# Graph network on one core: an edge stage planned in pairs of chunks, three far and two near per turn, instead of groups of four

## The chip, the cores and the metric

One core of a Trainium2 chip runs the whole program as one launch. The metric is the device time in microseconds; the figures given are the median of three runs, with the lowest and the highest.

## The reference

A graph of 6250 nodes with 128 features and 200000 edges (`src`, `dst`, sorted by `dst`) passes four graph layers, each followed by a residual sum and a layer norm. The change touches the last one, an attention over edges, and the step that plans its work:

```python
row, col = edge_index          # row = src, col = dst
h = relu(x[row] @ W1[:d] + x[col] @ W1[d:] + b1)
mask = sigmoid(h @ W2 + b2)[:, 0]
seg_sum = segment_sum(mask, row, num_segments=n)
w = mask / (seg_sum[row] + 1e-09)
agg = segment_sum(w[:, None] * x[col], row, num_segments=n)
out_emb = where((deg > 0)[:, None], 0.5 * x + 0.5 * agg, x)
return relu(out_emb @ Wl + bl)
```

## The kernel before, in words

The edges are sorted on the chip by the tile of 128 nodes that holds their `src` (`load_columns`, `rank_columns`, `permute_columns`, `bucket_ranges`). A **chunk** is 128 edges of one such tile. Each of the 49 tiles gets an even number of chunks, enough for its edges. Counted from the reference's inputs this gives 1614 chunks. A chunk is **near** when the `dst` nodes of its edges lie in two neighbouring tiles (828 chunks of the 1614), otherwise **far**.

`edge_attention` works in **turns**. For every chunk it needs `u` at the source node, plus, at the target node, `v` and the features `x`. The source part is a matmul of a one-hot matrix with the tile of `u` that stays in SBUF. The target part of a far chunk is gathered row by row from a table in DRAM by an indirect DMA of GpSimd (L1694, 128 rows of 1 KB). That of a near chunk comes from two more matmuls with two neighbouring tiles of `vx` (L1862, L1864). So a far chunk costs one gather, and a near chunk costs two extra matmuls of 256 columns. The operands are fp32, and one such matmul is two records in the profile ("x8" is four chunks).

In the kernel before, one turn is three **groups of four** chunks: two far groups (g = 0, 1) and a near one (g = 2), 12 chunks in all. In step t of the loop (`step` of each engine, buffers `h` alternate):

- PE, for each group: `lookups` of turn t (L1868, or L1862 to L1864 for the near group, into `psz` and `psv`), then `sums` of turn t-1 (L1879, into `psa`), which add the weighted rows up by source node.
- DVE: the one-hots of turn t+1 (L1774). Then, for each group, `z` = matmul + gathered rows (L1807), the adds of turn t-1 from `psa` to the accumulator (L1792, one per pair of chunks), the score with relu and weights (L1819, one per chunk), and the transposed one-hots of turn t+1 (L1778, L1781 for the near ones). For the near group the scores wait for a copy by ACT (`near_x`, L1906).
- ACT: for each group the sigmoid (L1908), then the weighted one-hots (L1914, one per chunk). Before those of the near group it makes `near_x`.
- SP: waits for plan row t+1, loads its numbers into registers, and fetches the broadcast rows for the transposed one-hots (L1708 for `low_rows`, L1709 for `near_rows`). Each time a group's gather of turn t has landed, it fetches the row numbers for that buffer's next gather (L1717). Last it fetches plan row t+2 (L1701).
- POOL: the gathers. It waits for the row numbers and, since the buffers alternate, for the sums of turn t-2.

Which chunks a turn works on stands in a **plan** in DRAM, one row of numbers per turn: tiles for PE, tiles of the sums for DVE, and first columns for SP and DVE. `plan_edges` makes it. Three consecutive groups out of `filled` need one near group (`room` = a third of the groups), and a group counts as near only if all its four chunks are near. With the reference's inputs there are 404 groups, of which 142 are near and 134 are taken as near. The 270 far ones are two per turn and the turns come in twos, so there are 68 trips or 136 turns, with 1088 gathers.

`plan_edges` first finds each group's slot on one partition with DVE operations over 415 elements (L810 to L827). PE turns slots and values into columns (L863, L866, L867). DVE makes one-hots of the slots (L843, L844), PE multiplies them with the values (L872, L875), and five DMAs write the plan (L790 to L794). Nothing else runs beside this step.

At the start of `edge_attention` DVE clears the accumulator (L1752), sets constants (L1754, L1755), copies the low bits of the source (L1756), makes the table row numbers (L1758 to L1760) and stages the first ones (L1767). Only then can the first gather start.

Of the kernel before, what the change touches and what calls it, by code (L numbers as in the profile page):

```python
# [4 lines left out]
F32 = mybir.dt.float32  # L5
# [8 lines left out]
P = 128  # L14
# [18 lines left out]
GROUPS = SC // 4  # L33
assert GROUPS * 21845 < 1 << 24
TURNS = 104
PLAN_ROWS = 212
STEP_W = 36
# [471 lines left out]
def bucket_ranges(nc, m, a):  # L509
# [4 lines left out]
    with ExitStack() as ctx:  # L514
# [10 lines left out]
        keys = sb("keys", [P, 5, NJ], F32)  # L525
# [226 lines left out]
def plan_edges(nc, m):  # L752

    BLK = [(b, min(P, GROUPS - b)) for b in range(0, GROUPS, P)]
    NB4 = len(BLK)
    with ExitStack() as ctx:
        sb = lambda n, s, d=F32: ctx.enter_context(nc.sbuf_tensor("pl_" + n, s, d))
        sem = lambda n: nc.alloc_semaphore("pl_" + n)  # L760
        line = sb("line", [1, 3, SCP])
        ordinal = sb("ordinal", [1, GROUPS])
        narrow, upto, near, taken = (sb(n, [1, GROUPS]) for n in ("narrow", "upto", "near", "taken"))
        to_near, to_far = sb("near_slot", [1, GROUPS]), sb("far_slot", [1, GROUPS])
        half, trips = sb("half", [1, 1]), sb("trips", [1, 1], I32)
        filled, filled_i = sb("filled", [1, 1]), sb("filled_int", [1, 1], I32)
        room, room_i = sb("room", [1, 1]), sb("room_int", [1, 1], I32)
        column = sb("column", [P, NB4])
        axis = sb("axis", [P, 4 * TURNS])
        slots = sb("slots", [P, NB4, 2])  # L770
        of_far, of_near = sb("of_far", [P, NB4, 5]), sb("of_near", [P, NB4, 9])
        far_hot, near_hot = sb("far_hot", [P, NB4, 4 * TURNS]), sb("near_hot", [P, NB4, 2 * TURNS])
        plan = sb("plan", [TURNS, 2, 19], I32)
        none = sb("none", [P, 2 * STEP_W], I32)
        psv = ctx.enter_context(nc.psum_tensor("pl_values_ps", [P, NB4, 16], F32))
        psf = ctx.enter_context(nc.psum_tensor("pl_far_ps", [P, 512], F32))
        psn = ctx.enter_context(nc.psum_tensor("pl_near_ps", [P, 512], F32))
        s_line, s_const, s_none, s_v, s_slots, s_values, s_hots, s_rows, s_plan, s_put = (
            sem(n) for n in ("line", "const", "none", "v", "slots", "values", "hots", "rows", "plan", "put"))
# [74 lines left out]

        @block.tensor
        def _(pe):
            pe.wait_ge(s_line, 16)
            one = m.ones[0:1, 0:1]
            for i, (b, n) in enumerate(BLK):
                for a in (0, 1):  # L860
# [750 lines left out]


def edge_attention(nc, m):

# [474 lines left out]
```

## Time and profile before

| | us |
|---|---|
| median of 3 runs | 4251.69 |
| lowest, highest | 4246.45, 4258.07 |
| the profiled execution's own time | 4245.02 |
| its span in the profile | 4243.3 |
| PE busy, share of the span | 3502.5, 83% |
| DVE busy | 3012.9, 71% |
| ACT busy | 2154.5, 51% |
| POOL busy | 1538.0, 36% |
| mean granted TensorE clock | 0.89 of 2.4 GHz |

The profiled execution is 1.7 us longer than its span and 6.7 us below the median. The shares are averages over stages with different limits, so the edge stage (from 2708 us to about 4150 us) and the plan step (775 to 813 us) are read on their own. "L1868" is a line of the kernel before; "PEld" is the weight load; "issue" is idle time for which the profile shows no releaser. SPq is SP's instruction queue, and its rows are the issuing of DMAs, not their transfer.

### The profile page before, as it was taken

How to read it: one execution, taken by the hardware profiler on the slowest of the kernel's cores; microseconds unless marked ns; L12 is line 12 of the kernel's file. 1: busy time of each engine (PE TensorE's matmuls, PEld its weight loads, DVE VectorE, ACT ScalarE, POOL GpSimd, SP SyncE). 2: the span in 40 equal slices, each digit the busy share in tenths (PEclk: the TensorE clock that was granted, in tenths of full speed). 3: DMA queues.
4: the chain of work that ended last, by engine and by line, in shares of the span. 5: the costliest groups of instructions: out<-in, count | busy, mean ns of one | idle time of the engine just before them, and what ended most of it. 6: DMA issues, size and time to landing. Idle time of an engine off the chain costs nothing. (4 is left out here: it accounts for less than half of the span.)

```text
span 4243.3 us, 93850 instructions
## 1 busy us (share of the span) xinstructions
PE 3502.5 (83%) x20539; PEld 2389.7 (56%) x20540; DVE 3012.9 (71%) x11949; ACT 2154.5 (51%) x6858; POOL 1538.0 (36%) x1256
## 2 busy tenths in 40 slices
PE   4868883698889899995998898688888888888884
PEld 2357782333333344443445344588888888888883
DVE  8999997798888888886002101688888888887785
ACT  0068895256677788885002101455555555555554
POOL 0058884100000000001002001277777777777770
PEclk8855555699999999997999999899999999999996
DMA  2011113001111222221884786355555555555551
GB/s 49 1 10 14 15 17 78 18 26 44 62 70 79 88 96 88 101 92 45 327 304 157 278 303 212 118 151 153 153 151 151 151 151 154 150 150 151 150 148 41
DMA packets 276486, 498.39 MB, mean 117 GB/s; under 512 B 92440, under 2 KB 192943, under 8 KB 276255
## 3 DMA queue, kind: packets, MB, share of 16 engines
q1 hardware_dynamic: 209922, 347.11, 24.4%
q0 software_dynamic: 66336, 149.10, 12.8%
q14 instruction: 191, 1.56, 0.1%
q8 instruction: 37, 0.61, 0.1%
HBM read 391.18 MB, written 104.89 MB: 117 GB/s over the span
## 5 line engine op out<-in xcount | busy, mean ns | idle before, releaser
L1694 POOL DMA_INDIRECT xs<-edge_table,ea_row_stage x1088 | 1085.1, 997 | 345.6 <-issue 329.3
L1245 PE MATMUL a_agg_ps<-a_adj_ring,parts 128*128 128x512 f16 (+1 forms) x2548 | 523.5, 369 | 47.1 <-DMA a_adj_ring<-adjacency 47.0
L1914 ACT ACTIVATE slot_dst<-ea_onehot,ea_mask 128x128 f32<-128x128 f16 x1632 | 535.8, 399 | 13.2
L1044 PE MATMUL ab_agg_ps<-ab_adj_stage,parts 128*128 128x512 f16 x1911 | 529.9, 388 | 0.0
L1868 PE MATMUL ea_psz<-parts,ea_onehot_t 128*128 x2176 | 307.7, 286 | 200.6 <-issue 182.5
L449 ACT ACTIVATE dst_step<-iota,dst_low_bias 128x128 f16<-128x128 f16 x1188 | 358.6, 405 | 216.0 <-PEq L474 213.0
L429 POOL DMA_INDIRECT records<-both_parts,record_row x98 | 350.4, 3576 | 309.9 <-ACT both_parts L455 285.6
L1908 ACT ACTIVATE ea_mask<-ea_dot,b 128x4 f32<-128x4 f32 x408 | 121.3, 297 | 671.0 <-DVE slot_src L1819 666.3
L1385 POOL TENSOR_TENSOR parts<-xs,parts 128x896 f16<-128x896 f32 x7 | 13.2, 1882 | 1226.7 <-ACT parts L1379 1226.7
L1879 PE MATMUL ea_psa<-xs,slot_dst 128*128 128x129 f32 x3264 | 437.5, 278 | 2.5 <-ACT slot_dst L1914 2.5
L1117 ACT ACTIVATE ab_src_off<-iota,ab_neg_src 128x128 f16<-128x128 f16 x712 | 282.2, 396 | 304.1 <-PE ab_adj_ps L1065 141.1
L1245 PEld LDWEIGHTS a_agg_ps<-a_adj_ring,parts 128*128 128x128 f16 x2548 | 242.1, 98 | 328.6 <-DMA a_adj_ring<-adjacency 48.0
L1879 PEld LDWEIGHTS ea_psa<-xs,slot_dst 128*128 128x128 f32 x3264 | 413.8, 194 | 9.8 <-DVE agg_t L1792 2.1
L1868 PEld LDWEIGHTS ea_psz<-parts,ea_onehot_t 128*128 128x128 f32 x2176 | 271.5, 196 | 225.6 <-issue 225.6
L1012 DVE TENSOR_SCALAR ab_dst_hot_middle<-iota,slot_dst 128x512 f16<-128x512 f16 x1218 | 395.0, 349 | 0.0
L1151 ACT ACTIVATE ab_adj_stage<-ab_adj_ps 128x512 f16<-128x512 f32 x637 | 371.9, 605 | 16.4 <-PE ab_adj_ps L1070 14.7
L1065 PE MATMUL ab_adj_ps<-ab_dst_hot_middle,ab_src_hot_middle 128*128 128x512 f16 x1218 | 337.8, 383 | 16.3 <-DVE ab_dst_hot_middle L1012 6.5
L1864 PE MATMUL ea_psv<-vx,xs 128*128 x1088 | 325.0, 380 | 0.0
L1862 PE MATMUL ea_psv<-vx,xs 128*128 x1088 | 324.3, 380 | 0.6 <-DVE xs L1781 0.6
L1044 PEld LDWEIGHTS ab_agg_ps<-ab_adj_stage,parts 128*128 128x128 bf16 x1911 | 190.3, 100 | 228.4 <-issue 19.1
L1792 DVE TENSOR_TENSOR agg_t<-agg_t,ea_psa 128x129 f32 x816 | 230.8, 283 | 96.7 <-PE ea_psa L1879 93.3
L1056 PE MATMUL ab_adj_ps<-ab_dst_hot_first,ab_src_hot_first 128*128 128x512 f16 x637 | 218.5, 391 | 84.7 <-DVE ab_dst_hot_first L1012 50.3
(387 smaller groups left out, 6433.5 us busy)
## 6 DMA issues: line engine op xcount, KB each, us to landing
a_adj_ring<-adjacency SPq DMA_DIRECT2D x182, 896.0 KB, 4.6
ea_low_rows<-low_rows SPq DMA_DIRECT2D x411, 128.0 KB
adjacency<-ab_adj_stage SPq DMA_DIRECT2D x91, 512.0 KB, 2.6
adjacency<-ab_adj_stage SPq DMA_DIRECT2D x91, 384.0 KB, 2.3
ea_near_rows<-near_rows SPq DMA_DIRECT2D x137, 128.0 KB
xs<-edge_table,ea_row_stage POOLq DMA_INDIRECT x1088
edge_table<-vx SPq DMA_DIRECT2D x12, 512.0 KB, 2.9
ea_row_stage<-row_columns SPq DMA_DIRECT2D x272, 2.0 KB
```

The lines of the kernel that those rows point to most:

```text
L429: nc.gpsimd.indirect_dma_start(m.rec[q % 2], bass.IndirectOffsetOnAxis(ap=rows[:, q:q + 1], axis=0), both[:, q, :], None, compute_op=ALU.a ...
L449: ins = nc.scalar.activation(step[:, h, k, :], m.iota128h[:, :], ACT.Sign, bias=m.lo_bias[:, bass.ds(n * K + k, 1)])
L1012: return nc.vector.tensor_scalar(dst[:, k, :], m.iota512[:, :], float(t * SPAN), m.slot_dst[:, bass.ds(c, 1)], ALU.add, ALU.is_equal)
L1044: ins = nc.tensor.matmul(agg_ps[:, :], lhs(r, t), stage[:, k, :], start=start and r == 0, stop=stop and r == parts - 1)
L1065: nc.tensor.matmul(ps[:, k, :], src_m[:, k, :], dst_m[:, k, :], start=False, stop=False).then_inc(s_used_m[k], 1)
L1151: nc.scalar.activation(stage[:, k, :], ps[:, k, :], ACT.Copy, accum_out=col(m.out_deg, n * TG + k)).then_inc(s_taken[k], 1)
L1245: ins = nc.tensor.matmul(ps[:, h, 0:width], lhs(r, t), ring[:, g % SLOTS, k * DB:k * DB + width], start=t == 0 and r == 0, stop=t == NT - ...
L1694: nc.gpsimd.indirect_dma_start(got[:, h, g, k, 0:ROW], None, m.table, bass.IndirectOffsetOnAxis(ap=row_s[:, h, g, k:k + 1], axis=0)).then_ ...
L1864: ins = nc.tensor.matmul(psv[:, k, :, :].rearrange("p c d -> p (c d)"), hot_d[:, 1, k, :], pair(1), start=False, stop=True)
L1868: ins = nc.tensor.matmul(psz[:, g, k, :], hot_t[:, g, k, :], of(m.u, tile_at(tiles[k])), start=True, stop=True)
L1879: ins = nc.tensor.matmul(psa[:, g, k // 2, 0:AW], hot_m[:, g, k, :], what, start=k % 2 == 0, stop=k % 2 == 1)
L1914: ins = nc.scalar.activation(hot_m[:, g, k, :], hot[:, h, g, :, k], ACT.Copy, scale=mask[:, g, k:k + 1])
```

## The change

The unit of the plan is a pair of chunks. A turn has five pairs: far group 0 with two pairs (4 chunks), far group 1 with one pair (2 chunks), and the near group with two pairs (4 chunks). That is 10 chunks, 6 far and 4 near, where it was 12, 8 far and 4 near. A pair counts as near if both chunks are near. From the reference's inputs there are 807 pairs, 337 of them near. `room` is 807 * 409 >> 10 = 322, which leaves 485 far pairs. Turns are (485 + 5) / 6 = 81 trips, or 162 turns, with 162 * 6 = 972 gathers and 162 * 4 = 648 near chunks (before 544).

The two chunks of a pair lie in one tile, so a plan row holds one tile per pair: PE loads 9 numbers instead of 16, DVE 10 instead of 16, SP 8 instead of 6. The broadcast rows are fetched by pair: five DMAs of `low_rows` and two of `near_rows`, each of 128 x 512 B, where there were three and one of 128 x 1 KB. The row numbers for the gathers take three DMAs instead of two.

The plan is made with one-hots of the slots of all chunks (13 blocks of 128 chunks by 840 far and 1120 near slots) which PE sums as the moving operand. The values (tile, first tile, column) are the two or three columns of weights. Eight DMAs with 280 short rows each write the plan from one to three partitions.

At the start of `edge_attention` the row numbers come first, and the clearing of the accumulator last.

```diff
-GROUPS = SC // 4
-TURNS = 104
-PLAN_ROWS = 212
-STEP_W = 36
+PAIRS = SC // 2
+TURNS = 280
+PLAN_ROWS = 284
+STEP_W = 32
...
 def plan_edges(nc, m):
...
-            sp.dma_start(rows_of(1, 0, 16), plan[:, :, 0:16]).then_inc(s_put, 16)
-            sp.dma_start(rows_of(2, 16, 28), plan[:, :, 0:12]).then_inc(s_put, 16)
...
+            sp.dma_start(to(1, 0, 3), far(1)).then_inc(s_put, 16)
+            sp.dma_start(to(2, 16, 3), far(1)).then_inc(s_put, 16)
+            sp.dma_start(to(0, 21, 3), far(0)).then_inc(s_put, 16)
...
-            ch(nc.vector.tensor_reduce(narrow[:, :], line[:, 2, 0:SC].rearrange("o (g k) -> o g k", k=4), AX.X, ALU.min))
+            ch(nc.vector.tensor_reduce(narrow[:, :], line[:, 0:SC].rearrange("o (g k) -> o g k", k=2), AX.X, ALU.min))
...
+            for j in range(NJ):
+                if j >= 4:
+                    dve.wait_ge(s_summed, j - 3)
+                nc.vector.tensor_scalar(far_hot[:, j % 4, :], axis[:, 0:FS], slots[:, j, 1:2], None, ALU.is_equal)
+                nc.vector.tensor_scalar(near_hot[:, j % 4, :], axis[:, :], slots[:, j, 0:1], None, ALU.is_equal).then_inc(s_hot, 1)
+            dve.wait_ge(s_summed, NJ)
+            nc.vector.tensor_scalar(far_v[:, :].rearrange("r (a s) -> r a s", a=2), psf[0:2, :, 0:FH], none_at[0:2, 0:1], None, ALU.add)
...
+            for j in range(NJ):
+                for a in (0, 1):
+                    ins = nc.tensor.matmul(psv[:, j, a:a + 1], slot[0:1, a, j * P:(j + 1) * P], one, start=True, stop=True)
...
+                for b in (0, 1):
+                    nc.tensor.matmul(psf[0:2, b, 0:FH], of_far[:, j, :], far_hot[:, j % 4, b * FH:(b + 1) * FH], start=j == 0, stop=j == NJ - 1)
+                for c, (c0, c1) in enumerate(CUTS):
+                    ins = nc.tensor.matmul(psn[0:3, c, 0:c1 - c0], of_near[:, j, :], near_hot[:, j % 4, c0:c1], start=j == 0, stop=j == NJ - 1)
...
 def edge_attention(nc, m):
+    FAR, NEARBY, KINDS = (0, 1), 2, (0, 1, 2)
+    SIZE, CHUNK, PAIR = (4, 2, 4), (0, 4, 6), (0, 2, 3)
+    CHUNKS, TWOS, FARS = 10, 5, 6
...
-                for g in KINDS:
-                    sp.dma_start(lo[:, h, g, :], m.low_rows[bass.ds(c, G), :]...broadcast_to([P, G * P])).then_inc(s_low[h], 16)
+                for q in range(TWOS):
+                    sp.dma_start(lo[:, h, q, :], rows_at(m.low_rows, base[q])).then_inc(s_low[h], 16)
+                for b, q in enumerate(twos(NEARBY)):
+                    sp.dma_start(rel[:, h, b, :], rows_at(m.near_rows, base[q])).then_inc(s_low[h], 16)
...
-                    nc.vector.tensor_tensor(hot[:, h, g, :, :], lo16[:, bass.ds(c, G)].unsqueeze(1).broadcast_to([P, P, G]), ramp[:, :, :], ALU.is_equal).then_inc(s_hot[g], 1)
+                    for q in twos(g):
+                        ins = nc.vector.tensor_tensor(hot[:, h, q, :, :], lo16[:, bass.ds(column(base[q]), 2)].unsqueeze(1).broadcast_to([P, P, 2]), ramp[:, :, :], ALU.is_equal)
+                    ins.then_inc(s_hot[g], 1)
...
-            nc.vector.memset(m.acc[:, :, :], 0.0)
-            dve.sem_inc(s_add, 16)
-            nc.vector.memset(near_x[:, :, :], 1.0)
...
+            nc.vector.memset(m.acc[:, :, :], 0.0)
+            dve.sem_inc(s_add, 16)
             turns(dve, step, after=after)
```

**SP, one step inside the loop of `edge_attention`**, from the broadcast rows to the next plan row. Before (`ISA` and `REGISTER_ALU` rows are address arithmetic):

```order
L1708 ISA
L1708 DMA ea_low_rows<-low_rows 128x512
L1708 ISA
L1708 DMA ea_low_rows<-low_rows 128x512
L1708 ISA
L1708 DMA ea_low_rows<-low_rows 128x512
L1709 DMA ea_near_rows<-near_rows 128x512
L1714 ISA
L1717 REGISTER_ALU
L1717 DMA ea_row_stage<-row_columns 128x4
L1717 REGISTER_ALU
L1717 DMA ea_row_stage<-row_columns 128x4
```

Now, from the fourth `low_rows` on (three more pairs of rows like the first two stand ahead):

```order
L1709 ISA
L1709 DMA ea_low_rows<-low_rows 128x256
L1709 ISA
L1709 DMA ea_low_rows<-low_rows 128x256
L1711 DMA ea_near_rows<-near_rows 128x256 x2
L1716 ISA
L1719 REGISTER_ALU
L1719 DMA ea_row_stage<-row_columns 128x2
L1719 REGISTER_ALU
L1719 DMA ea_row_stage<-row_columns 128x2
L1716 ISA
L1719 DMA ea_row_stage<-row_columns 128x2
```

Ten DMAs stand between two plan rows where six stood, all on SP's one queue.

**DVE, the start of `edge_attention`.** Before:

```order
L1752 MEMSET agg_t 128x6321
L1754 MEMSET xs 128x528
L1755 MEMSET xs 128x16x4
L1756 CAST ea_src_low<-slot_src 128x1664
L1758 CAST slot_dst<-slot_dst 128x1664
L1759 TENSOR_SCALAR slot_dst<-slot_dst 128x1664
L1760 TENSOR_SCALAR slot_dst<-slot_dst 128x1664
L1662 TENSOR_LOAD ea_steps
L1767 ISA
L1767 COPY ea_row_stage<-slot_dst 128x4
```

Now:

```order
L1756 CAST slot_dst<-slot_dst 128x1664
L1757 TENSOR_SCALAR slot_dst<-slot_dst 128x1664
L1758 TENSOR_SCALAR slot_dst<-slot_dst 128x1664
L1658 TENSOR_LOAD ea_steps
L1763 ISA
L1763 COPY ea_row_stage<-slot_dst 128x2
...
L1841 MEMSET xs 128x528
L1842 MEMSET xs 128x12x4
L1843 CAST ea_src_low<-slot_src 128x1664
...
L1778 TENSOR_SCALAR xs<-ea_near_rows,row_ids 128x512 x2
L1849 MEMSET agg_t 128x6321
```

The accumulator's clearing, two small memsets and one cast left the way of the first gather's row numbers (`ea_row_stage`). The clearing now stands between the first transposed one-hots and the one-hots of turn 1.

## Rows read from the trace of the kernel before

**Rows 1.** The page, costliest groups (part 5): the gathers of the edge stage.
```profile
L1694 POOL DMA_INDIRECT xs<-edge_table,ea_row_stage x1088 | 1085.1, 997 | 345.6 <-issue 329.3
```

**Rows 2.** One tile, `ea_psz`: count, duration ns min/median/max, first and last start us.
```profile
L1868 PE MATMUL ea_psz<-parts,ea_onehot_t x2176: 274/275/577, 2722.5 to 4142.9; 128*128 x198
```

**Rows 3.** Waits, 2800 to 4100 us: total us, times, longest us.
```profile
POOL xs L1694 <- issue: 301.8, 987, 1.2
...
PE ea_psz L1868 <- issue: 164.2, 121, 2.7
...
DVE ea_onehot_t L1778 <- DMA ea_near_rows<-near_rows: 7.2, 20, 1.3
```

**Rows 4.** Windows: us, busy (xcount) PE, PEld, DVE, ACT, POOL; PEclk, DMA, GB/s.
```profile
790.00:813.00 23.00, 12.24 (x68) 12.03 (x67) 3.87 (x26) 0.00 (x0) 0.00 (x0) 0.50 0.02 1
...
2300.00:2600.00 300.00, 269.47 (x1317) 135.71 (x1318) 39.01 (x172) 38.00 (x79) 17.97 (x10) 0.95 0.73 260
...
2700.00:4100.00 1400.00, 1204.44 (x8419) 1125.08 (x8420) 1123.01 (x5272) 707.98 (x2238) 1056.02 (x1059) 0.99 0.52 151
```

**Rows 5.** Timeline of PE, 2690 to 2760 us: start us, us, what, [idle before].
```profile
2744.36 0.60 PE L1862 MATMUL ea_psv<-vx,xs 128*128 x2
...
2748.70 1.05 PE L1879 MATMUL ea_psa<-xs,slot_dst 128*128 128x129 f32 x8
...
2749.60 1.11 PE L1868 MATMUL ea_psz<-parts,ea_onehot_t 128*128 x8
...
2758.83 1.15 PE L1868 MATMUL ea_psz<-parts,ea_onehot_t 128*128 x8 [0.20 <-issue]
```

**Rows 6.** Timeline of all engines, 2746 to 2772 us, same columns.
```profile
2750.27 0.29 DVE L1819 SCALAR_TENSOR_TENSOR slot_src<-ea_psv,w 128x128 f32<-128x128 f32 x1
...
2751.72 0.88 DVE L1781 TENSOR_SCALAR xs<-ea_near_rows,row_ids 128x512 f32<-128x512 f16 x2
...
2760.21 0.29 DVE L1819 SCALAR_TENSOR_TENSOR slot_src<-ea_psv,w 128x128 f32<-128x128 f32 x1 [0.99 <-ACT xs L1906]
...
2761.81 0.88 DVE L1781 TENSOR_SCALAR xs<-ea_near_rows,row_ids 128x512 f32<-128x512 f16 x2
...
2762.93 0.69 PE L1862 MATMUL ea_psv<-vx,xs 128*128 x2 [0.26 <-DVE xs L1781]
```

**Rows 7.** Timeline of the SP queue, 3304 to 3330 us.
```profile
3306.48 0.33 SPq L1717 DMA_DIRECT2D ea_row_stage<-row_columns  x1
3307.16 0.28 SPq L1701 DMA_DIRECT2D ea_steps<-plan_rows  x1
3309.93 1.39 SPq L1708 DMA_DIRECT2D ea_low_rows<-low_rows  x3
3311.41 0.38 SPq L1709 DMA_DIRECT2D ea_near_rows<-near_rows  x1
3312.13 5.34 SPq L1717 DMA_DIRECT2D ea_row_stage<-row_columns  x2
```

**Rows 8.** Timeline of the plan step and what follows it, 760 to 830 us.
```profile
777.82 12.40 PE L863 MATMUL pl_values_ps<-ones,pl_line 1*128 1x1 f32 x64 [12.97 <-DMA pl_line<-chunk_lines]
...
781.01 0.64 DVE L818 SCALAR_TENSOR_TENSOR pl_narrow<-pl_ordinal,pl_filled,pl_narrow 1x415 f32<-1x415 f32 x1
...
786.50 0.36 DVE L827 TENSOR_SCALAR pl_far_slot<-pl_far_slot 1x415 f32<-1x415 f32 x1
...
806.43 0.99 SPq L790 DMA_DIRECT2D plan_rows<-pl_plan  x1
...
809.89 0.25 SPq L794 DMA_DIRECT2D plan_rows<-pl_plan  x1
...
813.08 1.89 DVE L1014 TENSOR_SCALAR ab_neg_src<-slot_src 128x3328 f32<-128x3328 f32 x1 [6.74 <-PEq L2040]
...
816.90 0.87 DVE L1012 TENSOR_SCALAR ab_dst_hot_first<-iota,slot_dst 128x512 f16<-128x512 f16 x3
```

**Rows 9.** Timeline of the start of the edge stage, 2698 to 2740 us.
```profile
2709.22 5.33 DVE L1752 MEMSET agg_t<- 128x6321 f32 x1 [4.43 <-issue]
```

More of the change, by code:

```diff
@@ L760, in plan_edges @@
         sem = lambda n: nc.alloc_semaphore("pl_" + n)
[L761 to L776, printed above, removed]
@@ L777, in plan_edges @@
-        psn = ctx.enter_context(nc.psum_tensor("pl_near_ps", [P, 512], F32))
-        s_line, s_const, s_none, s_v, s_slots, s_values, s_hots, s_rows, s_plan, s_put = (
-            sem(n) for n in ("line", "const", "none", "v", "slots", "values", "hots", "rows", "plan", "put"))
+        line = sb("line", [1, SCP])
+        ordinal = sb("ordinal", [1, PAIRS])
+        narrow, upto, near, taken = (sb(n, [1, PAIRS]) for n in ("narrow", "upto", "near", "taken"))
+        to_near, to_far = sb("near_slot", [1, PAIRS]), sb("far_slot", [1, PAIRS])
@@ new lines, in plan_edges @@
+        far_v, near_v, near_e = sb("far_values", [2, FS], I32), sb("near_values", [3, NS], I32), sb("near_evens", [3, NS // 2], I32)
+        none = sb("none", [P, 4 * STEP_W], I32)
+        psv = ctx.enter_context(nc.psum_tensor("pl_values_ps", [P, NJ, 2], F32))
+        psf = ctx.enter_context(nc.psum_tensor("pl_far_ps", [P, 2, 512], F32))
+        psn = ctx.enter_context(nc.psum_tensor("pl_near_ps", [P, 3, 512], F32))
+        s_line, s_const, s_none, s_v, s_slots, s_values, s_hot, s_summed, s_plan, s_put = (
+            sem(n) for n in ("line", "const", "none", "v", "slots", "values", "hot", "summed", "plan", "put"))
@@ L842, in _ @@
-            for i in range(NB4):
-                nc.vector.tensor_scalar(far_hot[:, i, :], axis[:, :], slots[:, i, 1:2], None, ALU.is_equal)
-                ins = nc.vector.tensor_scalar(near_hot[:, i, :], axis[:, 0:2 * TURNS], slots[:, i, 0:1], None, ALU.is_equal)
-            ins.then_inc(s_hots, 1)
-            dve.wait_ge(s_rows, 1)
-            far = psf[0:TURNS, 0:20].rearrange("q (h a v) -> q h a v", h=2, a=2)
-            close = psn[0:TURNS, 0:18].rearrange("q (h v) -> q h v", h=2)
-            nc.vector.tensor_copy(plan[:, :, 0:8].rearrange("q h (a v) -> q h a v", a=2), far[:, :, :, 0:4])
@@ L1656, in edge_attention, with column @@
         s_got = [[sem(f"got{h}{g}") for g in FAR] for h in (0, 1)]
+        LOADS = TWOS + 2
+        chunks = lambda g: slice(CHUNK[g], CHUNK[g] + SIZE[g])
+        twos = lambda g: range(PAIR[g], PAIR[g] + SIZE[g] // 2)
         block = ctx.enter_context(nc.Block())
         def load(eng, h, c0, n):
-            return nc.values_load_multi_w_load_instructions(steps[0:1, h, c0:c0 + n], engines=(eng.engine,), min_val=0, max_val=SC + G,
+            return nc.values_load_multi_w_load_instructions(steps[0:1, h, c0:c0 + n], engines=(eng.engine,), min_val=0, max_val=SC,
                                                             skip_runtime_bounds_check_because="the plan holds tiles and columns")[1]
+        def column(v):
+            return nc.s_assert_within(v, 0, SC, skip_runtime_bounds_check_because="the plan holds columns")
         def tile_at(v, top=NT - 1):
```

263 lines of the change are left out of this document (133 added, 130 removed).

## Prediction, made before the changed kernel had run

> **What bounds the kernel now.** I read the page first. GpSimd's gathers are its costliest single group [rows 1]: 1088 gathers, 1085.1 us busy, 329.3 us of idle without a releaser between them. That is 0.997 + 0.303 = 1.30 us per gather, or 8 x 1.30 = 10.40 us a turn. The waits of a long steady stretch show the same gap, 301.8 us over 987 gathers, and hardly any other wait of POOL [rows 3]. The matmuls on `psz` start at 2722.5 and last at 4142.9 us [rows 2], so the stage runs 1420.4 us. After three slow turns at the start (2722.5 to 2758.8, 36.3 us [rows 2, 5]) the other 132 turns take 10.47 us each, allowing 1.9 us inside the last one. POOL fills 10.40 of these 10.47 us: the stage is bound by the issuing of gathers. TensorE is busy 1204.4 of 1400 us in it at a granted clock of 0.99 [rows 4], the upper of its two levels, and its own pause is 164.2 us over 121 turns, 1.36 us a turn, again without a releaser [rows 3].
>
> The turn is not much longer than the next limits. In the third turn POOL was not yet behind: PE went from one `psz` start to the next in 9.23 us, with 0.20 us idle [rows 5]. So twelve chunks cost PE 9.03 us, and its 1.36 us pauses are waiting, not work.
>
> The plan step stands alone in time. Its transposes start at 777.8 us and the next stage's first operation at 813.1 us [rows 8]; in its last 23 us PE works 12.2 and DVE 3.9, mostly in turn [rows 4]. What is added there is paid in full.
>
> **The edge stage, turn by turn.** The turns go from 136 to 162 (counted from the inputs), so the break-even turn is about 10.47 x 132 / 158 = 8.75 us. Five limits of the new turn:
>
> - POOL: 6 x 1.30 = 7.80 us.
> - PE: of the 9.03 us, the near lookups take 4.34 (2744.36 to 2748.70) and the near sums 0.90 (2748.70 to 2749.60) [rows 5]. That leaves 3.79 for 16 far lookups and sums, 0.237 each. Four fewer: 9.03 - 0.95 = 8.08 us.
> - The **near chain**. PE's near lookups and sums of a turn, ACT's `near_x`, DVE's near scores and transposed one-hots, then PE's next near lookups. From the rows: 4.34 us of lookups; 1.57 from the start of the sums over ACT's `near_x` to DVE's first near score (2748.70 to 2750.27); from there 2.33 to the end of L1781 (2750.27 to 2752.60), and 2.48 in the next turn (2760.21 to 2762.69); 0.24 until PE starts (2762.93, "DVE xs L1781" named as its releaser) [rows 5, 6]. Sum 8.5 to 8.6 us. The near group keeps its four chunks, so nothing of this chain gets shorter. Before, it hid under POOL.
> - The **SP chain**: from one plan row's issue to the next. Before: 2.77 us from L1701 to the first `low_rows` (landing and register load, 3307.16 to 3309.93), 1.48 to `near_rows`, 0.72 to the first row numbers, and 0.68 from the last row numbers to the plan row (3306.48 to 3307.16) [rows 7]. The three `low_rows` in 1.39 us are 0.53 apart. Now two more of them (1.06), a second `near_rows` (0.43, estimated from its 0.38 plus a gap), and two more steps between row numbers (0.5 and 0.6, estimated from the 0.53): 2.77 + 2.54 + 0.43 + 0.72 + 1.1 + 0.68 = 8.2 us. Two more values to load add under 0.1: 8.3 us.
> - DVE: 1123.0 us busy in 1400 [rows 4], 8.4 us for a turn of twelve chunks. Ten need between 7.0 us (if all its work goes by the chunk) and 8.4 (if five one-hots of 256 columns instead of three of 512 ate all the gain). I take 7.2; either way it stays under the near chain.
>
> The largest is the near chain; the SP chain and PE lie 0.3 and 0.5 us below, close enough that a late landing in one now and then reaches the other. I take 8.6 us a turn, the upper end of the near chain. Lower end 8.48; upper end 8.9, if the jitter adds 0.3.
>
> The start's three turns lose two gathers in each of the first two: 36.3 - 4 x 1.3 = 31.1 us. The stage is then 31.1 + 158 x 8.6 + 1.9 = 1391.8 us against 1420.4: **-28.6 us**. Each 0.1 us of turn is 16 us.
>
> **The start of the edge stage.** The memset of 5.33 us [rows 9] leaves the way of the first gather, with a memset of 528 columns and a cast of 1664 (at its rate of 6321 columns in 5.33 us 1.8 us more): up to 7.1 us. That memset now stands ahead of the one-hots of turn 1, while the gathers fly. I take **-6 us**; ends 0 and -8 (the first turns also begin earlier against their gathers).
>
> **The plan step.** The one-partition chain L818 to L827 (781.01 to 786.86) takes 5.85 us for 415 elements [rows 8]. With 830 it at most doubles, and three strided writes for one plain one add 1 to 2 us, while some 1.2 us of single-number work goes ahead of the line's arrival: +5 us, slots ready near 791. Then 26 transposing matmuls, of the kind that took 12.40 us for 32 [rows 8]: 10.1 us, to 801. The first one-hots take about 1 us. The sums move 13 x 1960 = 25480 columns: a window at clock 0.95 had 1317 matmuls of mostly 512 columns in 269.5 us, 0.205 us each [rows 4], so 10.2 us at the upper clock; the plan step before had clock 0.50, the lower level, so 20.4 us there. I take 16, to 818. The one-hots themselves (0.87 us for three of 512 columns at the next stage's start [rows 8], 0.6 to 1.1 us for 1960) hide behind them. Three us of copies from PSUM at the rate of 0.64 us for 415 elements [rows 8]. Eight DMAs: the five of before took 806.43 to 810.14, the first with 208 short rows 0.99 us; 280 rows cost about 1.2, so 9.6 us, to 831. Then 2.9 us as before (810.14 to 813.08). The next stage starts at 834 instead of 813: **+21 us**, ends +12 and +32.
>
> **Sum:** -28.6 - 6 + 21 = -13.6 us in the profiled execution, 4245.0 to 4231. That execution is 6.7 us below the median of the runs; against the median it is 4251.7 - 13.6 = 4238 us. Nothing else in the program changes.
>
> **A rule against the change.** The low rows were hardly waited for: 7.2 us in 20 waits over 1300 us [rows 3]. Each fetch now moves 64 KB instead of 128 KB, and there are seven instead of four. The Trainium skill (DMA: Bandwidth & Descriptors, "Rules for kernel authors") says to coalesce many small transfers, since below 64 KB one pays mostly overhead. The change sits just at that size and goes the other way. By the sum above the smaller fetches cost only SP's issue slots; by the rule their cost would be in the landing, and the second rival would hold. The trace has no 64 KB broadcast that could decide it.
>
> **Rivals.**
>
> 1. *Faster than I say:* the near chain runs at its lower end and the plan's sums at the upper clock. Turn 8.48, plan +15: 31.1 + 1339.8 + 1.9 = 1372.8, -47.6; total -38.6 us, 4213. For it: the rows 2.33 and 0.24 are measured; PE under solid columns may be granted the upper level. Against it: the plan step's engine work before held 0.50 throughout [rows 4].
> 2. *Slower:* SP becomes the bound. Ten DMAs per turn on one queue stand between two plan rows, and the last broadcast row is issued 1.5 us later in the chain, so DVE's transposed one-hots of the first group wait for it (the wait that is 7.2 us now), and with them the near scores behind. It decides from 8.75 us a turn: SP's chain 8.3 plus 0.5 of landing that comes after the issue. At 8.95 us: 31.1 + 1414.1 + 1.9 = 1447.1, +26.7; with -6 and +21 total +41.7 us, 4293. At 8.8 it is +18, 4270. For it: the SP chain is only 0.3 below the near chain. Against it: SP also issues while it has slack to run ahead.
> 3. *Not what it says:* if the 0.30 us between gathers were a wait for others, fewer gathers would not shorten the turn, and 162 turns of about 10 us would give 1620 us, +200, and with the rest about +215 us, 4467. The pause comes before nearly every gather (987 times, 0.31 us each, [rows 3]), not once a turn as a wait for another engine would, so I give it 0.02.
>
> **Chances.** My own case (turn 8.52 to 8.72, plan +15 to +27) 0.50; rival 1 0.22; rival 2 0.26; rival 3 0.02. 0.3% of this kernel is 12.8 us, about what a measurement can tell from no change. My case's centre lies almost on that line: 0.25 of its 0.50 goes to faster, 0.25 to the same. Rival 1 is all faster, 0.22; rival 2 begins inside the line, 0.05 same and 0.21 slower; rival 3 is slower. Faster 0.47, same 0.30, slower 0.23. My case's own range is 4220 to 4259; both sides hold chance, so the range runs from 4212 to 4284, into both rivals, and leaves 0.1 out at each end.
>
> **What would show it.** In the profile after: POOL's gathers with waits on `ea_psa` or row numbers between turns; PE waiting before L1862 for DVE's L1778 (the old L1781), 0.3 to 0.6 us a turn; the `psz` starts 8.6 us apart; SP issuing the plan row without waiting long for gathers; the next stage starting near 834 us. Wrong would be: POOL still without other waits, DVE waiting for `near_rows` every turn (rival 2), a turn over 8.75 us, or a plan step over 50 us.

## The result and the profile after

The changed kernel takes 4407.1 us (median of 4 runs, 4398.4 to 4409.3), the kernel before 4249.1 in 4 runs beside it: 1.036 of it, 95% interval 1.034 to 1.038. I had forecast 4238 us and a range up to 4284.

The table sets the two profiled executions against each other, in us. The plan step is taken from its first DMA to the first operation of the next stage, the edge stage from the first to the last `psz` start.

| stretch | before | after | difference | predicted |
|---|---|---|---|---|
| up to the plan step | 774.9 | 781.0 | +6.1 | 0 |
| plan step | 38.2 | 58.4 | +20.2 | +21 |
| from there to the first `psz` | 1909.4 | 1904.2 | -5.2 | -6 |
| edge stage | 1420.4 | 1560.9 | +140.5 | -28.6 |
| rest of the span | 100.4 | 101.5 | +1.1 | 0 |
| span | 4243.3 | 4406.0 | +162.7 | -13.6 |

The first line is no part of the change: the plan step of the kernels below, which differ only behind it, starts between 773.5 and 782.5 us. The loss is in the edge stage. It has 162 turns as counted, but they take 1560.9 / 162 = 9.63 us each instead of 8.6.

The groups of the page after that answer to [rows 1] and, for DVE's wait, to [rows 3]:

```profile
L1693 POOL DMA_INDIRECT xs<-edge_table,ea_row_stage x972 | 971.4, 999 | 596.2 <-issue 372.1
...
L1775 DVE TENSOR_SCALAR ea_onehot_t<-ea_low_rows,row_ids 128x512 f32<-128x512 f16 (+1 forms) x489 | 220.9, 452 | 230.1 <-DMA ea_near_rows<-near_rows 230.0
```

Eight gathers a turn are now six (972 in all) of the same 1.0 us, but POOL's idle time grew from 345.6 to 596.2 us: POOL no longer bounds the stage. DVE's transposed one-hots wait 230.0 us for `near_rows`. The waits of 2800 to 4100 us (total us, times, longest us), the window of [rows 3], say how often:

```profile
POOL xs L1693 <- issue: 308.3, 688, 4.9
DVE ea_onehot_t L1775 <- DMA ea_near_rows<-near_rows: 191.1, 133, 3.5
POOL xs L1693 <- PE ea_psa L1884: 171.2, 69, 5.2
...
PE ea_psz L1872 <- issue: 112.2, 121, 3.0
```

It was 7.2 us in 20 waits before. 133 waits in 1300 us at 9.63 us a turn is one in almost every turn: what the prediction named as the sign of its second rival. The same in the SP queue, as [rows 7]; the timeline of after from 3498 us:

```profile
3505.00 0.28 SPq L1700 DMA_DIRECT2D ea_steps<-plan_rows  x1
3509.21 2.41 SPq L1709 DMA_DIRECT2D ea_low_rows<-low_rows  x5
3511.71 0.85 SPq L1711 DMA_DIRECT2D ea_near_rows<-near_rows  x2
3512.82 1.42 SPq L1719 DMA_DIRECT2D ea_row_stage<-row_columns  x3
3514.59 0.28 SPq L1700 DMA_DIRECT2D ea_steps<-plan_rows  x1
```

From one plan row's issue (3505.00) to the first `low_rows` (3509.21) 4.21 us, to `near_rows` 2.50, to the row numbers 1.11, to the next plan row 1.77: 9.59 us. SP does not pause for gathers in it, where before it stood 5.34 us over two row numbers [rows 7]. Nor is it an odd turn: over 124 turns between 2900 and 4100 us the four parts average 4.12, 2.52, 1.15 and 1.86 us, 9.64 in all. All but the first term are as predicted (2.54, 1.15, 1.78). The first was 2.77 before (2.89 on average over 114 turns) and I left it there. What lies in it is a landing and a register load; the tile `ea_steps` of before, then of after, shows the loads of each engine (duration in ns: least, median, most):

```profile
L1662 DVEq TENSOR_LOAD <-ea_steps x138: 893/1100/1377, 2719.3 to 4152.0; - x138
L1662 SPq TENSOR_LOAD <-ea_steps x137: 721/882/918, 2709.1 to 4137.3; - x137
L1662 PEldq TENSOR_LOAD <-ea_steps x136: 1102/1105/1121, 2709.5 to 4137.2; - x136
```

```profile
L1658 DVEq TENSOR_LOAD <-ea_steps x164: 612/1066/1864, 2737.5 to 4314.3; - x164
L1658 SPq TENSOR_LOAD <-ea_steps x163: 1665/1832/1865, 2734.0 to 4301.1; - x163
L1658 PEldq TENSOR_LOAD <-ea_steps x162: 836/847/877, 2734.5 to 4301.1; - x162
```

SP loaded six values in 0.88 us; the changed kernel loads eight in 1.83. PE and DVE load more values (nine, ten) in 0.85 and 1.07 in the loop. DVE's longest, 1.864 us at 2737.5, is its one load of the same eight columns as SP's, ahead of the first turn, so the long time does not belong to SP.

### The profile page after: what moved, and what is told of

The parts are those of the page before. It is cut to its first block and busy times, and to the rows that moved or that the text cites. A ratio compares the mean times of both kernels' runs of the same rounds, so it can differ in the third digit from the quotient of the medians.

```text
span 4406.0 us, 98706 instructions
## 1 busy us (share of the span) xinstructions
PE 3624.9 (82%) x20896; PEld 2465.3 (56%) x20897; DVE 3060.3 (69%) x12519; ACT 2183.3 (50%) x6976; POOL 1423.1 (32%) x1140
## 3 DMA queue, kind: packets, MB, share of 16 engines
q0 software_dynamic: 60768, 133.89, 11.3%
## 5 line engine op out<-in xcount | busy, mean ns | idle before, releaser
L1693 POOL DMA_INDIRECT xs<-edge_table,ea_row_stage x972 | 971.4, 999 | 596.2 <-issue 372.1
L1920 ACT ACTIVATE slot_dst<-ea_onehot,ea_mask 128x128 f32<-128x128 f16 x1620 | 526.5, 391 | 15.8
L1913 ACT ACTIVATE ea_mask<-ea_dot,b 128x4 f32<-128x4 f32 (+1 forms) x486 | 144.3, 297 | 781.5 <-DVE slot_src L1817 771.2
L1884 PE MATMUL ea_psa<-xs,slot_dst 128*128 128x129 f32 x3240 | 447.0, 277 | 3.3 <-ACT slot_dst L1920 3.3
L1866 PE MATMUL ea_psv<-vx,xs 128*128 x1296 | 400.3, 390 | 50.5 <-DVE xs L1778 47.7
L1872 PE MATMUL ea_psz<-parts,ea_onehot_t 128*128 x1944 | 290.3, 287 | 164.3 <-issue 142.6
L1868 PE MATMUL ea_psv<-vx,xs 128*128 x1296 | 387.4, 381 | 0.0
L1775 DVE TENSOR_SCALAR ea_onehot_t<-ea_low_rows,row_ids 128x512 f32<-128x512 f16 (+1 forms) x489 | 220.9, 452 | 230.1 <-DMA ea_near_rows<-near_rows 230.0
L1872 PEld LDWEIGHTS ea_psz<-parts,ea_onehot_t 128*128 128x128 f32 x1944 | 247.2, 195 | 193.2 <-issue 193.0
```

Source lines behind the costliest of these rows:

```text
L1693: nc.gpsimd.indirect_dma_start(got[:, h, k, 0:ROW], None, m.table, bass.IndirectOffsetOnAxis(ap=row_s[:, h, k:k + 1], axis=0)).then_inc(s_ ...
L1866: nc.tensor.matmul(psv[:, k, :, :].rearrange("p c d -> p (c d)"), hot_d[:, 0, k, :], pair(0), start=True, stop=False)
L1868: ins = nc.tensor.matmul(psv[:, k, :, :].rearrange("p c d -> p (c d)"), hot_d[:, 1, k, :], pair(1), start=False, stop=True)
L1872: ins = nc.tensor.matmul(psz[:, g, k, :], hot_t[:, CHUNK[g] + k, :], of(m.u, tile_at(tiles[k // 2])), start=True, stop=True)
L1884: ins = nc.tensor.matmul(psa[:, g, k // 2, 0:AW], hot_m[:, c, :], what, start=k % 2 == 0, stop=k % 2 == 1)
L1920: ins = nc.scalar.activation(hot_m[:, c, :], hot[:, h, PAIR[g] + k // 2, :, k % 2], ACT.Copy, scale=mask[:, c:c + 1])
```

## Experiments

Theory A: SP's chain from plan row to plan row sets the turn at 9.6 us, and the slow load is the largest part of its excess. Theory B: the near chain is longer than I made it. Theory C: the seven 64 KB broadcasts land late whatever SP does. No kernel below leaves work out unless the text says so. "Turn" is the `psz` span over 162 (over 136 where the kernel before is edited).

### The load and the fetch

e1_load9, the changed kernel with nine values from column 20 for eight from column 21:

```diff
-                base = load(sp, slot, BASES, NEXT + 3 - BASES)
+                base = load(sp, slot, BASES - 1, NEXT + 4 - BASES)[1:]
```


> SP loads nine values from column 20 in place of eight from column 21 and ignores the first. If SP's chain from one fetch of a plan row to the next sets the turn (theory A) and this load is shorter (0.85 to 1.1 us instead of 1.83), each of 162 turns gets up to 0.95 us shorter, down to what the near group's chain allows (8.6 us by the prediction, from 9.58 now): 4250 to 4290. If the load stays at 1.8, or the near group's own work sets the turn (theory B), or the small broadcast transfers take their time on the DMA engines whatever SP does (theory C): 4395 to 4415.

e2_early, the changed kernel with the plan row fetched first:

```diff
                 sp.sem_inc(s_seen_sp, 1)
-                then = fetch_rows(1 - h, 1 - h)
-                fetch_next(then, h, i)
                 sp.wait_ge(s_read, t + 1)
...
                 fetch_steps(t + 2, h)
+                then = fetch_rows(1 - h, 1 - h)
+                fetch_next(then, h, i)
```


> SP fetches the plan row after next at the head of its step, ahead of the seven row transfers and the three small ones, instead of behind them; its landing (about 1.9 us from the start of the issue to SP's going on) then leaves SP's chain. Theory A: SP's chain falls from 9.58 to about 7.8 us, the next limit (near group, 8.6) sets the turn: 4245 to 4290, and DVE's wait for near_rows (192 us in the window from 2900 to 4200) falls under 50. Theory B or C: 4395 to 4415 and that wait stays.

e3_both has both edits:

> Both edits: the nine-value load and the early fetch. Theory A: SP's chain about 6.8 us, so the time is that of the next limit and stands within 15 us of the early fetch alone (4240 to 4285); POOL's idle time between gathers is then under 2 us a turn. If the fetch alone leaves SP the bound, this one is another 100 us or more faster than it. Theories B and C: 4395 to 4415.

| kernel | us | ratio to before, 95% interval | turn | DVE for `near_rows`, 2900 to 4100 us |
|---|---|---|---|---|
| changed | 4407.1 | 1.036 (1.034 to 1.038) | 9.63 | 177.5 |
| e1_load9 | 4272.3 | 1.005 (1.003 to 1.007) | 8.86 | 60.5 |
| e2_early | 4264.5 | 1.004 (1.003 to 1.006) | 8.77 | 46.2 |
| e3_both | 4244.3 | 0.999 (0.998 to 1.000) | 8.65 | 13.5 |

The load of e1_load9, from its tile `ea_steps`:

```profile
L1658 SPq TENSOR_LOAD <-ea_steps x163: 751/916/951, 2734.0 to 4174.9; - x163
```

One value more and one column earlier takes half the time, and 135 us of the kernel go. Moving the fetch, with the load as slow as before, takes 143 us. Both are what A expects; by B and C the time would have stayed at 4395 to 4415. The wait speaks against C too: the same seven broadcasts are hardly waited for once SP issues them earlier. In e1_load9 the four parts of SP's chain average 3.09, 2.52, 1.15 and 2.07 us, 8.83: SP still sets that turn, or nearly. Two signs named for e3_both missed: it is 20 us, not up to 15, below the early fetch alone, and POOL is idle 369.7 us in 1200, 2.7 us a turn instead of under 2.

### What makes a load slow

p_loads put fourteen more loads behind the last turn, without a use for their values:

> The changed kernel with fourteen more register loads of SP behind the last turn, of 1 to 10 values from columns 16 to 28 of a plan row; nothing else differs. In the changed kernel SP's load of eight values from column 21 takes 1.83 us; in the kernel before six values from column 28 took 0.88; PE's nine values from column 0 take 0.85 and DVE's ten from column 16 take 1.07. Theory 'start': a load is cut into pieces whose number depends on where it starts, so eight values from column 24 or 16 take under 0.9 us, eight from 21 take 1.8, and nine from 20 about 0.9 to 1.1. Theory 'count': eight values are slow wherever they start, 1.8 us each. Theory 'engine': all of SP's loads grow with the count, about 0.2 us for each value. The time grows by 12 to 20 us over the changed kernel's 4407.

It took 4397.5 us and its trace has the changed kernel's 163 loads and no more: unused loads had dropped out of the program, so it told nothing of the loads. p_loads2 uses every value:

```diff
+                for c0, n in [(21, 8), (20, 9), (20, 8), (22, 8), (24, 8), (16, 8), (21, 5), (21, 4), (21, 3), (26, 3), (21, 7), (22, 7), (16, 10)]:
+                    for v in load(sp, 0, c0, n):
+                        sp.dma_start(m.scratch[n_out:n_out + 1, :], m.row_cols[0:1, bass.ds(column(v), 2)]).then_inc(s_kept, 16)
+                        n_out += 1
```


> The register loads of the first attempt again, behind the last turn of the changed kernel, now each value used as the column of a small transfer so that the loads stay in the program: (first column, count) = (21,8) (20,9) (20,8) (22,8) (24,8) (16,8) (21,5) (21,4) (21,3) (26,3) (21,7) (22,7) (16,10). The nine-value load of the last runs took 0.92 us against 1.83 for eight from column 21. Theory 'start': (24,8) and (16,8) under 0.6, (21,8) 1.8, the others between. Theory 'count': every load of eight 1.8 us, whatever its start, and 7, 9 and 10 values 0.8 to 1.1. The time itself is longer than the changed kernel's by 40 to 60 us and tells nothing.

Six of them, (20,9), (20,8), (22,8), (24,8), (21,5) and (21,3), each the answer on `ea_steps` for a window around it:

```profile
L1659 SPq TENSOR_LOAD <-ea_steps x1: 1292/1292/1292, 4306.9 to 4306.9; - x1
...
L1659 SPq TENSOR_LOAD <-ea_steps x1: 1060/1060/1060, 4315.5 to 4315.5; - x1
...
L1659 SPq TENSOR_LOAD <-ea_steps x1: 2180/2180/2180, 4322.6 to 4322.6; - x1
...
L1659 SPq TENSOR_LOAD <-ea_steps x1: 1034/1034/1034, 4330.8 to 4330.8; - x1
...
L1659 SPq TENSOR_LOAD <-ea_steps x1: 1577/1577/1577, 4344.9 to 4344.9; - x1
...
L1659 SPq TENSOR_LOAD <-ea_steps x1: 1191/1191/1191, 4355.3 to 4355.3; - x1
```

Eight values take 1.06, 1.03 and 1.03 us from columns 20, 24 and 16, but 2.18 from column 22. From columns 21, 22 and 26, 3, 4, 5, 7 and 8 values took 1.19, 1.38, 1.58, 1.98 and 2.18 us: 0.20 us for each value. All but the first of the thirteen, (21,8) with 1.84, stand behind a train of small DMAs and include about 0.37 us for that (nine from column 20 take 1.29 here, 0.92 in the loop). So it is the start that counts: the quick ones are multiples of four; 22 and 26 are even and slow, 20 is no multiple of eight and quick. The expectation had eight aligned values under 0.6 us; without the 0.37 they take 0.66 to 0.69. Beyond eight the aligned loads grow again, 1.29 us for nine and 1.48 for ten from column 16.

The Trainium skill (Runtime: NRT & Kernel Launch, "Instruction fetch mechanics") gives about 200 ns for each register, "even for bulk", for the runtime's own loads, which read HBM; the loads here read SBUF. The slope behind the slow starts agrees. The aligned starts do not, and there the measurement decides: eight values cost 1.03 to 1.06 us, about what the slow starts' line gives for two.

One reading fits the loads of both kernels, as an estimate from their figures and tested no further: from an aligned start four values go as one piece and the rest one by one, from any other start all go one by one, and a load takes about 0.2 us and 0.2 more for each piece (within 0.12 us). Two pieces: DVE's last load, five from column 16, 0.61 us. Three: six from 28 in 0.88 and 0.89, nine from 0 in 0.85, nine from 20 in 0.92. Four: DVE's ten and sixteen from 16, 1.07 and 1.10, PE's sixteen from 0, 1.10. Eight: eight from 21, 1.83 on SP and 1.86 on DVE.

### The old kernel with the early fetch

b1_early is e2_early's edit on the kernel before.

> The kernel before with the early fetch of the plan row alone. There SP waited 3.9 us a turn for the gathers (478.1 us in 124 waits), so theory A (SP bounds only the changed kernel, POOL's gathers the one before) says no change: 4238 to 4262. If SP's chain set the pace of the old kernel too, it would fall by 100 us or more.

4238.1 us, 0.998 (0.997 to 0.999), at the edge of the range: about 10 us less, where A said none. Its turn is (4131.4 - 2727.0) / 136 = 10.33 us instead of 10.44. The waits of 2900 to 4100 us in b1_early:

```profile
POOL xs L1694 <- issue: 265.7, 872, 0.3
...
POOL xs L1694 <- PE ea_psa L1879: 10.4, 34, 0.3
```

POOL's pauses are now 0.30 us each and never longer. In the kernel before the longest was 1.2 [rows 3]: a little of what I had read as the pause between gathers was waiting, and SP had a small share in it.

### What holds 8.65 us

With SP out of the way the turn is what I had forecast. Is it the near chain? Two edits tried to shorten that chain, on the changed kernel (a1_near) and on e3_both (f1_near): two buffers for the near group's copied rows, and its additions last.

```diff
-        near_x = spare[:, GOT:GOT + NEAR_W].rearrange("p (k w) -> p k w", k=G)
+        near_x = spare[:, GOT:GOT + 2 * NEAR_W].rearrange("p (h k w) -> p h k w", h=2, k=G)
...
                     transposed(g, 1 - h, t)
+                    if adds and g == NEARBY:
+                        adds[0]()
+                        adds[1]()
```


> The changed kernel, SP as it is, with the near group's copied rows in two buffers, so that ScalarE's copies and VectorE's scores of the near pairs no longer wait for the sums of the turn before, and the two additions of the near group behind its scores. It shortens the near group's chain by 1.2 to 1.5 us a turn (VectorE's wait for those sums) and leaves SP's chain. Theory A: no gain, 4390 to 4412. Theory B (the near group sets the turn): 1.0 us or more a turn off, under 4270.

> The same edit on the kernel with both SP edits (4244 us). There VectorE waited 168 us in 133 waits for these sums. If the near group's chain is what holds that kernel at 8.6 us a turn, the turn falls to the next limit, TensorE or POOL, 8.1 to 8.3 us: 4170 to 4205. If TensorE, busy 95% of that stage, is already the bound, or the turn is held by SP: 4230 to 4250.

Both lost: 4458.4 us (1.049, 1.047 to 1.052) and 4461.0 (1.050, 1.048 to 1.052), each with turns of 9.99 us, so neither speaks for or against the near chain. I had missed a wait. From the waits of 2900 to 4100 us in f1_near, then e3_both:

```profile
DVE ea_onehot L1770 <- issue: 171.5, 120, 1.7
...
DVE slot_src L1817 <- ACT xs L1914: 148.3, 120, 1.2
```

```profile
DVE agg_t L1789 <- PE ea_psa L1884: 168.0, 133, 1.5
...
PE ea_psv L1866 <- DVE xs L1778: 63.0, 139, 1.8
...
DVE ea_onehot L1770 <- issue: 17.3, 70, 0.3
```

DVE's wait for the sums (168.0 us) has become one for ScalarE's copies, and a second has come, ahead of the first one-hots. Each addition waits for the one before it on DVE's own semaphore. When they stand last, nothing is queued while DVE loads the next turn's ten values (1.07 us). One turn of f1_near, the timeline and the load, then the same load in e3_both:

```profile
3521.49 0.72 DVE L1789 TENSOR_TENSOR agg_t<-agg_t,ea_psa 128x129 f32 x2
...
3523.41 1.10 DVE L1770 TENSOR_TENSOR ea_onehot<-ea_src_low,ea_ramp 128x256 f16<-128x256 f16 x5 [1.20 <-issue]
...
L1658 DVEq TENSOR_LOAD <-ea_steps x1: 1066/1066/1066, 3522.1 to 3522.1; - x1
```

```profile
3528.35 0.88 DVE L1778 TENSOR_SCALAR xs<-ea_near_rows,row_ids 128x512 f32<-128x512 f16 x2
3529.49 1.10 DVE L1770 TENSOR_TENSOR ea_onehot<-ea_src_low,ea_ramp 128x256 f16<-128x256 f16 x5 [0.26 <-issue]
...
L1658 DVEq TENSOR_LOAD <-ea_steps x1: 1073/1073/1073, 3528.1 to 3528.1; - x1
```

In f1_near the load starts as the last addition ends, and DVE stands 1.20 us. In e3_both it starts at 3528.1, under operations that last until 3529.23, and DVE stands 0.26. Putting the additions between the scores tests this (g1_again, on e3_both):

```diff
+                        if k == 1 and adds and g == NEARBY:
+                            adds[0]()
+                        if k == (3 if g == NEARBY else 1) and len(adds) > 1:
                             adds[1]()
```


> Two buffers for the near group's rows, the additions between its scores. If the additions' place behind the one-hots was what cost 216 us (VectorE's load of ten values with nothing queued ahead of it), its idle time before the one-hots is under 30 us and the time 4200 to 4250; below 4225 the near group's chain was the limit at 8.6 us a turn. If the two buffers cost the time: over 4400.

4240.6 us, 0.997 (0.996 to 0.998), idle before the one-hots 27.5 us: the place of the additions had cost the 216 us. But the gain over e3_both is small, and by the sign named for it (below 4225) the near chain is not shown as the limit: DVE waits for ScalarE's copies as long as it had for the sums, 163.9 us in 139 waits. Three kernels leave work out of e3_both: two of the first far group's four lookups (x1_again) and two of the near group's four single lookups (x4_ring), both from the third turn on, and one of six gathers, with the counts of its waits (x3_again). e3_again is their control. A single lookup of the near group is its matmul with the tile of `u`, so it belongs to the source node; the expectation of x4_ring calls it the destination's row.

```diff
-                    for k in range(SIZE[g]):
+                    for k in range(SIZE[g] if g or seen < 2 else 2):
```
```diff
-                    for k in range(CHUNK[g], CHUNK[g] + SIZE[g]):
+                    for k in range(CHUNK[g], CHUNK[g] + SIZE[g] - g):
```
```diff
+                        if seen < 2 or k < 2:
                             nc.tensor.matmul(psv[:, k, 0, :], hot_t[:, CHUNK[g] + k, :], of(m.u, tile_at(tiles[k // 2])), start=False, stop=False)
```


> The kernel with both SP edits once more, as the control for the three behind it: the last three kernels and the kernel before beside them ran on a chip on which the kernel before took 4640 us, so their times can't be set against 4244. On a chip that gives the kernel before 4250 us, this one again takes 4235 to 4255 (ratio 0.997 to 1.001).

> Two of the first far group's four lookup matmuls left out in every turn from the third on: TensorE 0.55 us less a turn outside the near group's chain. TensorE as the bound: 70 to 90 us below the control. A chain through the engines as the bound: under 25 us.

> One of six gathers left out: POOL issues 1.3 us less a turn. POOL as the bound: over 100 us below the control. The near group's chain as the bound, with POOL at 7.8 under it: under 15 us.

> The kernel with both SP edits, less two of the four single lookups (of the destination's row) in the near group of every turn from the third on. As many matmuls go as in x1_again, which gained nothing, but these stand in the near group's ring: one-hots on VectorE, twelve matmuls on TensorE, copies on ScalarE, scores and the next one-hots on VectorE. If that ring sets the turn (8.6 us by the prediction), 0.35 to 0.6 us a turn go, 4155 to 4190. If something else does: within 15 us of 4245, as x1_again.

| kernel | us | ratio to before | turn |
|---|---|---|---|
| e3_again | 4245.8 | 0.998 (0.998 to 0.999) | 8.67 |
| x1_again | 4245.8 | 0.998 (0.997 to 0.999) | 8.67 |
| x3_again | 4232.8 | 0.995 (0.994 to 0.997) | 8.60 |
| x4_ring | 4222.7 | 0.992 (0.990 to 0.993) | 8.50 |

Two lookups of TensorE outside the near group are worth nothing, 1.3 us of POOL's issuing 0.07 us a turn. Two matmuls taken out of the near group's ring are worth 0.17 (x4_ring ran on another chip than its control; by the ratios to the kernel before it is 0.7% of the time). So the ring holds the turn, but loosely: 23 us came (29 by the ratios), where I expected 55 to 90. Where the rest went is only read from the waits: DVE waits 33.3 us for `near_rows` and 31.9 for ScalarE's copies in 1200, where the control has 14.6 and 6.2. h1_copies, on g1_again, moves ScalarE's two copies of that ring ahead of its multiplications of the second far group:

```diff
-                    if g == NEARBY:
-                        act.wait_ge(s_u[g], t + 1)
...
                     act.wait_ge(s_mask[g], t + 1)
+                    if g == 1:
+                        act.wait_ge(s_u[NEARBY], t + 1)
+                        if seen >= 2:
+                            act.wait_ge(s_agg[NEARBY], t - 1)
+                        for a in (0, 2):
+                            nc.scalar.activation(near_x[:, h, a:a + 2, 0:D], psv[:, a:a + 2, 1, :], ACT.Copy).then_inc(s_near_x, 1)
```


> On g1_again (4240.6): ScalarE's two copies of the near group's rows are put ahead of its two one-hot multiplications of the second far group instead of behind them. VectorE waited for these copies 163.9 us in 139 waits there. If the near ring sets the turn, the scores start 0.3 to 0.6 us earlier: 4140 to 4200 and faster than both kernels. If not: 4230 to 4250.

4215.9 us, 0.990 (0.989 to 0.992), turn 8.47: faster than both kernels, but short of the 4140 to 4200 that the near ring as the limit was to give. The waits of 2900 to 4100 us show DVE's wait for the copies down from 163.9 to 92.4 us, and `near_rows` back as one of the limits beside it:

```profile
DVE slot_src L1817 <- ACT xs L1916: 92.4, 140, 0.9
POOL xs L1693 <- PE ea_psa L1886: 57.1, 63, 3.2
...
DVE ea_onehot_t L1775 <- DMA ea_near_rows<-near_rows: 49.6, 58, 3.3
```

Does the pair unit gain by itself, then? b2_all has these edits (early fetch, two buffers, additions, copies) on the kernel before:

> The kernel before with the three edits that took the changed kernel from 4407 to 4216: the early fetch of the plan row, two buffers for the near group's rows with the additions between its scores, and ScalarE's copies ahead of the second far group's multiplications. With groups of four POOL issues eight gathers of 1.30 us a turn, and b1_early stands at 4238. If POOL bounds it, nothing more is gained: 4228 to 4245, and the pair unit is worth 15 to 30 us once its own chains are out of the way. If the edits help here as much as there, under 4220, and the pair unit is worth nothing.

4256.7 us, 1.002 (1.001 to 1.003), with DVE now waiting 174.3 us for gathers (61.2 in the kernel before). That is outside both ranges. The edits that bring the pairs to 4216 bring groups of four nothing, and leave them 19 us behind the early fetch alone; why they lose is not shown. The fastest kernel here has the pair unit, 22 us below the best that groups of four gave (4238, on another chip); by the ratios, 0.990 and 0.998, it is 0.7%. Other orders of the work with groups of four were not tried.

## Why the prediction was wrong, by its steps

The window of 2900 to 4100 us in e3_both (us, busy (xcount) of PE, PEld, DVE, ACT, POOL; granted clock, DMA share, GB/s), for the second point:

```profile
2900.00:4100.00 1200.00, 1136.75 (x7782) 1053.33 (x7781) 993.00 (x5141) 652.93 (x2085) 830.47 (x834) 1.00 0.54 145
```

- **What bounds the kernel before:** POOL's issuing, right but for the 0.1 us a turn of b1_early.
- **POOL 7.80, PE 8.08, DVE 7.2:** right. In the window DVE is busy 0.83 of a turn of 8.65, 7.2 us, and PE 0.95, 8.2; POOL's gathers still take 1.0 us each. Neither PE nor POOL is the bound, as x1_again and x3_again show; no run took work from DVE.
- **Near chain 8.5 to 8.6:** what e3_both reached, 8.65, with the sign named for it: PE waits for DVE's L1778 in 139 turns, 63.0 us or 0.45 a turn. That this chain is what holds it is shown in part (x4_ring, h1_copies); how the other limits share in it stays open, and so does how much of the agreement is luck.
- **SP chain 8.3:** the step that failed, and in it the sentence "Two more values to load add under 0.1". They added 0.95 (0.88 to 1.83), because the load starts at column 21 now and started at 28 before. Another 0.27 is in the landing of the plan row, which I left as it was: from 2800 to 4100 us SP waited 118.1 us in 123 waits for it before, 160.5 in 130 after, 1.23 us each instead of 0.96. Why it lands later is not shown. And the 2.77 was one turn's, 0.12 below the average of 2.89. The sum of 8.24 with 0.95, 0.27 and 0.12 gives 9.58; measured 9.63.
- **Rival 2** was the right mechanism, with its sign (DVE waiting for `near_rows` in every turn) and its price too low: I priced it at 8.95 us a turn, +42 us or 4293, with 0.5 us of landing, and ended the range at 4284. The slow load and the later plan row made it 9.63.
- **The rule on 64 KB transfers**, which the prediction takes from the Trainium skill, did not decide: with SP earlier the same seven transfers were waited for 13.5 us in 1200, the four of 128 KB before 6.7.
- **Plan step +21:** +20.2, in part by luck, as the terms were off against each other. This execution begins the step 6.1 us later, so the terms compare as lengths. The chain on one partition took 17.0 us from the step's start to 798.0, where the prediction had 16.1 to 791 (the memset of a line of 3328 on one partition alone took 2.83 us). The transposes took 11.3, not 10.1, the copies 3.7, not 3, and the time behind the last DMA 3.9, not 2.9. Against that the sums took 13.8 us, not 16, and the eight DMAs 7.5, not 9.6. The rows:

```profile
781.91 2.83 DVE L813 MEMSET pl_slot<- 1x3328 f32 x1 [0.63 <-issue]
...
787.84 1.07 DVE L826 SCALAR_TENSOR_TENSOR pl_narrow<-pl_ordinal,pl_filled,pl_narrow 1x830 f32<-1x830 f32 x1
...
797.39 0.58 DVE L836 TENSOR_SCALAR pl_slot<-pl_far_slot 1x830 f32<-1x830 f32 x1
...
798.09 11.25 PE L863 MATMUL pl_values_ps<-ones,pl_slot 1*128 1x1 f32 x52 [27.12 <-DVEq L837]
...
810.50 0.86 PE L868 MATMUL pl_far_ps<-pl_far_hot,pl_of_far 128*2 128x420 f16 x2 [1.17 <-DVE pl_near_hot L849]
...
824.36 1.08 DVE L851 TENSOR_SCALAR pl_far_values<-pl_far_ps,pl_none_at 2x840 int32<-2x840 f32 x1 [2.47 <-PE pl_near_ps L870]
...
828.01 0.93 SPq L792 DMA_DIRECT2D plan_rows<-pl_far_values  x1
...
834.79 0.75 SPq L799 DMA_DIRECT2D plan_rows<-pl_near_evens  x1
839.39 1.89 DVE L1010 TENSOR_SCALAR ab_neg_src<-slot_src 128x3328 f32<-128x3328 f32 x1 [11.46 <-PEq L2046]
```

- **Start -6:** -5.2.

## What to carry to other kernels

An engine that runs ahead in the old kernel has its own serial chain; when a change gives it more steps, write that chain down with every row measured, register loads and landings included, and test what is closest to it before trusting a gap of 0.3 us. Start a multi-value register load at a multiple of four columns (of 4-byte values), and fetch a loop's next table row ahead of the work that uses the present one. An operation that waits on its own engine's semaphore should not stand last ahead of a load: whatever would have hidden the load has then drained.

## What the runs showed of the hardware

- A register load of eight values takes 2.18 us from column 22 and 1.03 to 1.06 from columns 16, 20 and 24, behind the same train of DMAs (in the loop, from column 21, 1.83). From columns 21, 22 and 26 each value costs 0.20 us.
- g1_adds, x1_pe and x3_pool, the first tries of three kernels above, ran on a chip that gave the kernel before 4640.6 us instead of 4250. On it they took 4683.6 (1.009), 4689.3 (1.010) and 4511.6 (0.972). What was expected of them was set against the 4244 us of e3_both, which did not run there, so it is neither met nor missed. But x3_pool, with a gather less, stands over 170 us below the other two, where a gather less was worth 13 us elsewhere; why is not shown. g1_adds is as fast as the others up to its first `psz` (2745.9 us), and its turns then take 11.39 us. One row of the tile `ea_low_rows`, SP's moves ahead of each fetch, in g1_adds and then in e3_both on another chip (ns: least, median, most):

```profile
L1709 SPq MOVE ea_low_rows<-low_rows x815: 1/29/721, 2736.6 to 4592.9; - x163
```

```profile
L1709 SPq MOVE ea_low_rows<-low_rows x815: 29/29/29, 2731.7 to 4140.4; - x163
```

What was expected of g1_adds:

> The last edit cost 216 us where it should have gained: VectorE stood idle 1.2 to 1.7 us ahead of each turn's first one-hots (185.8 us in 130 waits, 17 before). My reading: the near group's additions, put last, wait on VectorE's own semaphore, so its queue is empty when it loads the next turn's ten values (1.07 us) and nothing hides that load. Here the two buffers stay, but the additions stand between the near group's scores (after the second and the fourth), so three one-hot operations are again queued ahead of the load. If that reading holds, the idle time before the one-hots is gone (under 30 us) and the time is 4244 or below: 4200 to 4244 if the near group's chain was the limit at 8.6 us a turn, 4235 to 4250 if it was not. If the two buffers are what cost the time (later copies on ScalarE), it stays over 4400.

The median of the moves is the same, but single moves take up to 0.72 us instead of 0.03. The Trainium skill (Runtime: NRT & Kernel Launch, "Instruction fetch mechanics") says that a taken branch can make an engine wait for its next instructions; whether that is it, on one chip and not on others, no run here shows. What it means for reading: those three are compared with nothing above.
